# Attention B: TensorE takes the score and first-pass products of two blocks together, then the fp32 products of the two blocks ahead of them

## What is computed

```python
x = x + attn_a(layernorm(x))      # relative positions, softmax over all 2048 keys
x = x + ffn(layernorm(x))         # 256 -> 1024 -> 256, relu
x = x + attn_b(layernorm(x))      # causal, below
x = x + ffn(layernorm(x))

def attn_b(x, Wq, bq, Wk, bk, Wv, bv, Wo, bo):
    q, k, v = heads(x @ Wq.T + bq), heads(x @ Wk.T + bk), heads(x @ Wv.T + bv)
    scores = q @ k.T / 4                    # 2048 x 2048 a head
    scores[key > query] = -inf
    out = softmax(scores) @ v
    return merge(out) @ Wo.T + bo
```

## Time and profile before

| | us |
|---|---|
| median of three runs (10728.02 to 10788.41) | 10734.49 |
| the profiled execution | 10788.76 |
| its span | 10787.0 |
| PE busy | 9252.8 (86%) |
| ACT busy | 5986.2 (55%) |
| DVE busy | 5702.9 (53%) |
| POOL busy | 2784.2 (26%) |
| mean granted TensorE clock | 0.935 |

### The profile page before, as it was taken

How to read it: one execution, slowest core, us unless ns; L and a number is a source line. 1 busy time by engine, 2 the same in 40 slices (tenths; PEclk the granted TensorE clock), 3 DMA queues, 4 the chain that set the end, 5 groups by cost and what they waited for, 6 DMA issues and landing times. The chain is left out here.

```text
span 10787.0 us, 254980 instructions
## 1 busy us (share of the span) xinstructions
PE 9252.8 (86%) x89696; PEld 5643.9 (52%) x89696; DVE 5702.9 (53%) x11468; ACT 5986.2 (55%) x10813; POOL 2784.2 (26%) x2893
## 2 busy tenths in 40 slices
PE   5888889899688888989968888889987888888999
PEld 3666666334466666633546556653344565665335
DVE  3655663553355556356346556636634565663563
ACT  3666664454466666435446666634535666662454
POOL 2333332000233333200023333320003333332000
PEclk7999999889899999979979999998998999998799
DMA  6999993110699999211069999921107999991010
GB/s 233 382 362 366 375 383 115 59 30 14 238 372 367 366 373 372 104 48 30 14 248 382 368 363 380 382 91 31 30 22 286 367 379 361 374 376 64 25 30 22
DMA packets 748147, 2476.67 MB, mean 230 GB/s; under 512 B 114080, under 2 KB 136096, under 8 KB 746528
## 3 DMA queue, kind: packets, MB, share of 16 engines
q1 hardware_dynamic: 746784, 2459.12, 61.9%
HBM read 1276.14 MB, written 1181.76 MB: 228 GB/s over the span
## 5 line engine op out<-in xcount | busy, mean ns | idle before, releaser
L695 DVE CUSTOM_DVE_ANT_0 z<-sc,z 128x1024 f32<-128x1024 f32 x2048 | 2496.2, 1220 | 1861.1 <-DMA z<-rel_rows 1598.2
L753 POOL TENSOR_SCALAR z<-z,nmax 128x1024 f32<-128x1024 f32 x2048 | 2276.2, 1123 | 4039.5 <-DVE nmax L705 4039.5
L668 ACT ACTIVATE pT<-rg 128x512 f32<-128x512 f32 x4096 | 2448.7, 598 | 748.6 <-PE rg L578 689.8
L578 PE MATMUL rg<-ident,z 128*128 128x128 f32 x16384 | 2537.1, 278 | 74.3 <-issue 66.7
L676 ACT ACTIVATE rel<-rg 128x512 f32<-128x512 f32 x3072 | 1720.8, 596 | 1404.8 <-PE rg L559 1400.8
L559 PE MATMUL rg<-pos_s,qv_s 96*128 96x512 bf16 x4096 | 1592.7, 396 | 1017.1 <-DVE rel L730 898.0
L578 PEld LDWEIGHTS rg<-ident,z 128*128 128x128 f32 x16384 | 2001.8, 143 | 787.5 <-ACT rel L676 291.4
L984 ACT ACTIVATE pT<-rg 128x512 f32<-128x512 f32 (+3 forms) x2560 | 1358.6, 533 | 1042.7 <-PE rg L913 589.3
L1000 DVE TENSOR_REDUCE mx_b<-sc 128x1 f32<-128x1024 f32 (+7 forms) x1024 | 1013.3, 991 | 788.5 <-PE sc L890 401.8
L559 PEld LDWEIGHTS rg<-pos_s,qv_s 96*128 96x128 bf16 x4096 | 478.9, 118 | 1492.7 <-DVE rel L730 1145.6
L599 PE MATMUL op<-pT,xnT 128*32 128x128 f32 x32768 | 1130.0, 279 | 0.0
(11 more groups left out here) (106 smaller groups left out, 7872.8 us busy)
## 6 DMA issues: line engine op xcount, KB each, us to landing
rel_rows<-rel SPq DMA_DIRECT2D x2048, 512.0 KB, 7.1
z<-rel_rows SPq DMA_DIRECT2D x2048, 512.0 KB, 7.1
v_heads<-rel SPq DMA_DIRECT2D x8, 4096.0 KB, 12.5
xnT<-v_heads SPq DMA_DIRECT2D x128, 256.0 KB, 3.3
qv_s<-qv_parts SPq DMA_DIRECT2D x384, 64.0 KB, 6.3
pos_s<-pos_parts SPq DMA_DIRECT2D x384, 64.0 KB, 7.3
xnT<-qu_parts SPq DMA_DIRECT2D x384, 64.0 KB, 6.4
z<-qu_parts SPq DMA_DIRECT2D x384, 64.0 KB, 2.2
```

The lines of the kernel that those rows point to most:

```text
L578: mm = e.transpose(rg[:, T_BANK[q], (j - 4 * q) * P:(j - 4 * q + 1) * P], z[:, n % RING, j * P:(j + 1) * P], ident[:, :])
L668: e.activation(pT[:, t % 2, q * CH:(q + 1) * CH], rg[:, T_BANK[q], :], ACT.Exp, scale=SCALE).then_inc(p_ready[q], 1)
L695: e.tensor_tensor_reduce(out=zs, in0=scf[:, 2 * half * CH:2 * (half + 1) * CH], in1=zs, scale=1.0, scalar=-3.0e38, op0=ALU.add, op1=ALU.ma ...
L753: e.tensor_scalar(zs, zs, 1.0, nmax[:, n % 2:n % 2 + 1], ALU.mult, ALU.add).then_inc(AA[done], 1)
```

## The change

PE's step is now run for every second i and does two blocks: the score products of blocks i and i+1, the sub pieces i+14 and i+15 of the next head, then `values` of blocks i-2 and i-1. `turn_max` stands behind the `values` of step 32, `turn_out` in the step after the one in which the group ended. DVE follows the same pairs; ACT copies the turned maxima one block later.

```diff
-ST_LEAD = 1
+PAIR = 2
-OUT_LAG = 3
+OUT_LAG = 2
@@ rotated
-                step(p, at, n, i + LAG, here)
+                if i % PAIR == 0:
+                    step(p, at, n, i + LAG, here)
@@
-        def sub_at(n, i):
-            u = i + EARLY
-            return n + 1 + u // NBLK, u % NBLK
+        def subs_at(n, i):
+            return [(n + 1 + u // NBLK, u % NBLK) for u in range(i + EARLY, i + EARLY + PAIR)]
+        def blocks_at(n, i):
+            return [(n + k // NBLK, k % NBLK) for k in range(i, i + PAIR)]
+        def groups_at(n, i):
+            return [(m, g) for m, k in blocks_at(n, i) for g in range(NG) if m >= 0 and k == G_END[g] - 1]
@@ pe_attn_b, lead_in
-                scores(at, 0, 0, True)
-                for i in range(LAG):
+                for i in range(0, LAG, PAIR):
@@ pe_attn_b, step
-                m, k = n + (i + ST_LEAD) // NBLK, (i + ST_LEAD) % NBLK
-                if here(m):
-                    scores(at, m, k, False)
-                h, u = sub_at(n, i)
-                if here(h):
-                    sub_piece(at, h, u, False)
+                for m, k in blocks_at(n, i):
+                    if here(m):
+                        scores(at, m, k, n + i == 0)
+                for h, u in subs_at(n, i):
+                    if here(h):
+                        sub_piece(at, h, u, False)
+                for m, k in blocks_at(n, i - PAIR):
+                    if i >= PAIR and here(m):
+                        values(at, m, k)
                 if i == TURN_STEP and here(n + 1):
                     e.wait_ge(BB["out_read"], at.groups + (n * NG + NG + 1))
                     turn_max(at, n + 1)
-                m, k = n + (i - 1) // NBLK, (i - 1) % NBLK
-                if i and here(m):
-                    values(at, m, k)
-                for g in range(NG):
-                    if (i - OUT_LAG - G_END[g]) in (0, NBLK):
-                        m = n + (i - OUT_LAG - G_END[g]) // NBLK
-                        if here(m):
-                            turn_out(at, m, g)
+                for m, g in groups_at(n, i - PAIR - OUT_LAG):
+                    if here(m):
+                        turn_out(at, m, g)
@@ act_attn_b, step
-                if i == TURN_STEP and here(n + 1):
+                if i == TURN_STEP + 1 and here(n + 1):
                     copy_max(at, n + 1)
@@ dve_attn_b, lead_in and step
-                for i in range(LAG):
+                for i in range(0, LAG, PAIR):
-                h, u = sub_at(n, i)
-                if here(h) and SUBS[u][2] == PIECES[SUBS[u][0]][2]:
-                    largest(at, h, SUBS[u][0])
+                for h, u in subs_at(n, i):
+                    if here(h) and SUBS[u][2] == PIECES[SUBS[u][0]][2]:
+                        largest(at, h, SUBS[u][0])
...
+                for m, g in groups_at(n, i - PAIR):
+                    if here(m):
+                        take(at, m, g)
+                for m, g in groups_at(n, i - PAIR - OUT_LAG):
+                    if here(m):
+                        normalise(p, at, m, g)
```

## The result

The changed kernel takes 10409.08 us, the median of four runs (10395.19 to 10419.44), against 10746.57 us before (four runs, 10728.02 to 10788.41): ratio 0.9676, 95% interval 0.9646 to 0.9707. By the medians that is 337 us less, 3.1%.

What follows compares the result with a forecast made beforehand. PE's start-to-start time was taken to bound attention B; 55.6 heads x 3.5 = 195 us, plus 43 at half clock, less 5 at batch ends, gave 233 us saved: 10502 us from the median, range 10435 to 10612.

Steps and rivals of the forecast that it cites:

- PE's starts bound attention B: Attention B's four stretches last as long as PE's instructions need from start to start, plus small waits; 36.16 us a head.
- Entry 0.09 and exit 0.14 go once a pair: Around the fp32 groups: one entry and exit per two blocks instead of two, saving 0.23 us a pair at full clock.
- the open bound: Second fp32 group of a pair, with its own wait: costs 0.22 us (taken) or 0.36.
- The waits grow from 0.43 to 1.54 us a head: Sub pieces wait for reductions on their reused half of `sc` at row tiles 1, 9, 10, 11, 12; 1.1 more.
- The 0.15 added at tile 11: Allowance in row tile 11's wait for a short reduction and division ahead on DVE; could be 0 to 0.5 us.
- ACT is covered by 0.19 us a pair, and holds every other pair in the last head: Paired exponentials finish 0.19 us early, except each batch's last head, every other pair held to 1.36; some 5 us lost.
- The sum: Attention B: 195 us at full clock plus 43 at half, less 5 at batch ends: 233 us saved.
- the half-clock term: Half-clock time in the stretches, 422 us, taken as 136 pairs each 0.32 us shorter: 43 us saved.
- The slower rival: Longer waits drop attention B's clock to 1.2 GHz; with 20 more heads at half clock 10961 us; chance 0.05.
- The second group does not stream: Rival: second fp32 group's weight loads stand open, so a pair saves only 0.09 us; 10630 us; chance 0.10.

Runs made afterwards that it cites:

- e1: Changed kernel with PE's order inside a pair undone (score, sub piece, fp32 group block by block), other changes kept; 10778.8 us, ratio to before 0.9995.
- e5: Changed kernel with every row-maximum reduction taken over only the first 128 columns of its piece; 10258.4 us.
- e0: The kernel before, unchanged, run once more with a second profile; 10750.8 us.
- e9: e1 with each block's four fp32 products in 32-column groups replaced by two 128-column fp32 products on the full array; 10624.5 us.
- e3: Changed kernel, interleaved in the first head of each group of four, paired in the other three; 10647.6 us, ratio to before 0.9859.
- e2: Changed kernel, paired only in the first head of each group of four, other three interleaved; 10581.0 us, ratio to before 0.9814.
- e4: e1 with score and sub piece products issued twice in the first head of each group of four; 10898.4 us.
- e7: Changed kernel; in each group's first head, every other pair's second score product also waits for the first's exponential; 10548.5 us.

## Why the prediction was right or wrong

- *PE's starts bound attention B*: right. DVE has the same busy time, ACT's is somewhat lower, and PE's order alone explains the result (e1).
- *Entry 0.09 and exit 0.14 go once a pair*: right. The plain pair was forecast at 1.55 and measured 1.54. That the second group's wait costs nothing was the open bound; it costs nothing.
- *The waits grow from 0.43 to 1.54 us a head*: right in sum (1.50 by e5). Place by place, in PE's starts after the change against the same transition without a wait: row tile 9 0.30 (0.29 forecast), tile 10 0.16 (0.14), tile 11 0.27 (0.41), tile 12 0.35 (0.35), tile 1 0.38 (0.35). The 0.15 added at tile 11 for a late DVE was not there.
- *ACT is covered by 0.19 us a pair, and holds every other pair in the last head*: right, as the end of the first stretch shows, where one pair (2480.78 to its fp32 group) takes 0.79 us to get there and the next 0.53 (in the first, the exponential on the bank that is reused ends at 2481.19 and the second score product starts at 2481.25):

```profile
2480.78 0.86 PE L921 MATMUL rg<-z 99*128 99x512 bf16 x2
2481.57 0.64 PE L936 MATMUL rg<-pT,xnT 128*32 128x128 f32 x16
...
2482.31 0.60 PE L921 MATMUL rg<-z 99*128 99x512 bf16 x2
2482.84 0.65 PE L936 MATMUL rg<-pT,xnT 128*32 128x128 f32 x16
```

- *The sum*: 233 us for the order, measured 233 by the balance above. That the two agree to the microsecond is in part luck: a head at full clock gave 3.73 us instead of 3.5, so 207 us instead of 195, and the 6.8 heads' worth at half clock gave 25 by the same balance instead of 43 - 5. **The step that failed is the half-clock term**: "the half-clock part is 422 / 3.11 = 136 pairs". It held the time at half clock as given by the kernel before and only made its pairs shorter; likewise "how long the clock stays at half behind each loop edge ... moves a run by some 30 us". The four stretches were 424 us at half clock before and 109 after, worth 132 us on top of the 233 (103 with e0's 355 us); the forecast's 43 for pairs at half clock is part of the 233. The stretches were to be 55 to 60 us shorter each and were 77 to 108. The rows spoke for a question there: at half clock PE was as busy as ever and the clock stayed down for 14 us behind one edge and 61 behind another. The forecast took this for variation from run to run, and its range, which ends at 10435, left no room for a gain.
- *The slower rival*: wrong in sign. It let longer waits bring the clock down. The waits came, but in every profile here each record of half clock within the stretches begins at a loop edge or before the stretch does. The price of half clock that it used, 2.79 us a pair, was about right (2.83 by rows).
- *The second group does not stream*: refuted. All loads here use all 128 rows, and two groups take 0.57 - 0.14 = 0.43 us. PE's weight loads (PEld) of the plain pair above show it directly:

```profile
2012.98 0.38 PEld L936 LDWEIGHTS op<-pT,xnT 128*32 128x32 f32 x16 [0.42 <-issue]
```

  The sixteen loads of both groups follow each other within 0.38 us, the second group's while products of the first still run. So the sentence of the Trainium skill (TensorE: Matmul & The Clock Gate, The mechanism) that weight loads overlap running matmuls only where row groups differ does not hold here. The same section also lets a load into a background weight buffer be pulled ahead; no row tells whether that is what happens.

## What to carry to other kernels

Group TensorE's work by the array's shape, not by precision: each passage to 32-column groups and back cost 0.23 us here at full clock, and four products in the groups stream in 0.22 us, the time of one such fp32 product on the full array (e9). When a change packs an engine more tightly, list every buffer that is reused and compare its chain (product, reduction, product: 1.81 us) with the new distance; all five waits came out of that sum within 0.14 us, and ordering long and short pieces removed nearly all of them. And treat time at half clock as something that the code behind an idle gap sets, not as a constant: read the granted clock by stretch, and ask what the changed kernel does right behind each gap.

## What the runs showed of the hardware that was not expected

- Behind the idle gaps at a loop edge (1 to 4 us each), half clock lasted 7 to 14 us wherever the head behind was paired and had no added waits (7 to 24 with them), and 10 to 72 us, differently each time, where the array changed shape for each block. PE was busy for 66 of 70 us in the windows of both that are shown.
- An order with no change of shape in its steps had it back after 3 to 10 us (e9). But the first pass alone, without changes of shape too, stayed at half clock for all of its 34.5 us, in which PE was busy for 25.7.
- The spread of the runs follows: 10395 to 10419 with pairs, 10720 to 10832 before beside e1 to e3. The unsteady part of the kernel before was its time at half clock: the mean granted clock of those runs goes from 0.940 and 0.941 in the two fastest to 0.930 and 0.928 in the two slowest.
- That the order behind the gap sets how long half clock lasts is shown (e1, e2, e3). By which property of the order stays open: neither the mean streaming share nor the number of changes a microsecond puts all runs in order at the edges (e4, e7), and at a stretch's start activity alone did help (e4, e5).
